# First layer: dense counting up to chunk 1150 instead of 1000, flushed in groups of four tiles instead of twenty

## What is computed

```
head = entity_emb[edge_index[0]]          # source
tail = entity_emb[edge_index[1]]          # destination
att_scores = sigmoid(concat(head, rel[edge_type]) @ att_w + att_b)
aggr_emb = segment_sum(att_scores * tail, edge_index[0], num_segments=N)
out = tanh(aggr_emb @ W_w.T + W_b)
x = layernorm(x + out)
```

## Time and profile before

| | before |
|---|---|
| median of three runs | 11344.98 us (11343.02 to 11346.07) |
| the profiled execution | 11343.15 us |
| its span, first to last instruction | 11341.4 us |
| first layer's indirect DMAs on POOL (L681) | 2125, from 143.6 to 4116.6 us |
| busy share of the span | PE 72%, DVE 68%, ACT 47%, POOL 74% |
| TensorE's granted clock, mean | 0.787 |

### The profile page before, as it was taken

How to read it: one execution, slowest core, us unless ns; L and a number is a source line. 1 busy time by engine, 2 the same in 40 slices (tenths; PEclk the granted TensorE clock), 3 DMA queues, 4 the chain that set the end, 5 groups by cost and what they waited for, 6 DMA issues and landing times. The chain is left out here.

```text
span 11341.4 us, 169992 instructions
## 1 busy us (share of the span) xinstructions
PE 8140.4 (72%) x50598; PEld 5841.4 (52%) x50599; DVE 7676.4 (68%) x18686; ACT 5286.9 (47%) x11630; POOL 8397.3 (74%) x7474
## 2 busy tenths in 40 slices
PE   3777777767777744555656679888888698888887
PEld 2545555555555532444545555555545555555445
DVE  6776666666665538866666559877776598777765
ACT  2644444434333314443333338765544387655442
POOL 4888888888888845777777737777777577777775
PEclk6756666666666656777787869999999799999997
DMA  5343333333333331111111111111111111111111
GB/s 146 37 48 39 38 37 38 38 38 39 38 39 38 39 71 45 29 29 29 29 29 28 27 28 30 30 29 29 29 28 27 35 30 29 30 29 29 28 27 32
DMA packets 690515, 416.79 MB, mean 37 GB/s; under 512 B 488171, under 2 KB 599947, under 8 KB 688344
## 3 DMA queue, kind: packets, MB, share of 16 engines
q0 software_dynamic: 479520, 263.96, 17.9%
q1 hardware_dynamic: 209208, 141.70, 4.7%
q10 hardware_dynamic: 880, 0.23, 0.0%
HBM read 294.68 MB, written 110.67 MB: 36 GB/s over the span
## 5 line engine op out<-in xcount | busy, mean ns | idle before, releaser
L744 POOL DMA_INDIRECT mem<-xt,mem x5325 | 5042.0, 947 | 1680.6 <-issue 1619.7
L681 POOL DMA_INDIRECT table<-mem,idx x2125 | 3305.8, 1556 | 741.9 <-issue 636.6
L1048 PE MATMUL ps<-mem 128*128 128x392 f32 (+5 forms) x6750 | 2707.5, 518 | 224.0 <-DVE mem L1561 106.5
L1561 DVE TENSOR_SCALAR mem<-ps,mem 128x392 f32<-128x392 f32 (+5 forms) x4050 | 2459.2, 627 | 0.0
L1575 DVE TENSOR_TENSOR mem<-mem,ps 128x392 f32 (+2 forms) x3150 | 1805.4, 573 | 851.3 <-PE ps L1048 631.3
L867 ACT ACTIVATE mem<-iota_f,mem 128x128 f32<-128x128 f32 x4050 | 1272.4, 390 | 2242.8 <-PE ps L1048 2231.8
L1081 PE MATMUL ps<-mem 128*64 128x64 f32 (+1 forms) x10650 | 954.8, 243 | 1468.0 <-DMA mem<-xt,mem 1467.3
L1060 PEld LDWEIGHTS ps<-mem,xs 128*64 128x64 f32 (+1 forms) x16464 | 1606.1, 152 | 495.9 <-issue 461.2
L1081 PEld LDWEIGHTS ps<-mem 128*64 128x64 f32 (+1 forms) x10650 | 800.0, 153 | 1958.9 <-DMA mem<-xt,mem 1864.4
L1060 PE MATMUL ps<-mem,xs 128*64 128x94 f32 (+1 forms) x16464 | 1758.6, 265 | 4.5 <-DVE acc L1581 4.5
L1048 PEld LDWEIGHTS ps<-mem 128*128 128x128 f32 (+1 forms) x6750 | 1094.9, 180 | 890.3 <-issue 428.8
(11 more groups left out here) (172 smaller groups left out, 7509.4 us busy)
## 6 DMA issues: line engine op xcount, KB each, us to landing
mem<-xt,mem POOLq DMA_INDIRECT x5325, 2.4
mem<-key_rows SPq DMA_DIRECT2D x425, 160.0 KB, 3.3
table<-mem,idx POOLq DMA_INDIRECT x2125, 3.1
table<-mem POOLq DMA_DIRECT2D x3, 6304.0 KB, 41.0
mem<-table SPq DMA_DIRECT2D x42, 448.0 KB, 5.2
mem<-in_x_dram SPq DMA_DIRECT2D x403, 16.0 KB, 2.0
xt<-xs SPq DMA_DIRECT2D x6, 1024.0 KB
mem<-in_x_dram SPq DMA_DIRECT2D x300, 1.2 KB
```

The costliest lines, as they stand in the source:

```text
L681: pool.indirect_dma_start(out=tables[i % NTAB][:, :], out_offset=bass.IndirectOffsetOnAxis(ap=idx[:, i % (IDXS * GC):i % (IDXS * GC) + 1], ...
L744: pool.indirect_dma_start(out=gbuf[:, o:o + F], out_offset=None, in_=xt[l][:, :], in_offset=bass.IndirectOffsetOnAxis(ap=src_q[q % 2].bitc ...
L1048: last = pe.matmul(ps_d[b % PSD][:, 0:w], lo_l[:, r * P:(r + 1) * P], blk_l[:, r * DT:r * DT + w], start=(k == 0), stop=(k == parts - 1))
L1561: ins = v.tensor_scalar(blk_l[:, r * DT:r * DT + w], iota_p[:, 0:w], kd_q[q % 2][:, at + k:at + k + 1], None, ALU.is_equal)
```

## The change

`C0` rises from 1000 to 1150 and `UZ` falls from 5 to 1; the cost of a zone in the call of `slots` goes from 11.0 to 2.2, so that the cost of a unit stays 2.2. A small row of segment bases moves (32 instead of 64 elements behind its neighbour), with an assertion that all fits.

```
-C0 = 1000
+C0 = 1150
 G00 = C0 // GC
 NT0 = NG - G00
...
-UZ = 5
+UZ = 1
...
 BLOCK0_END, ZONE0_END = slots(SEG_OF0, [0.13 * k * d + 0.24 * d for (_, k), d in zip(BLOCKS[:NB0], ROWS_OF)],
-                              11.0, NU // UZ, NT0, 8)
+                              2.2, NU // UZ, NT0, 8)
...
-        sbase, sbase0 = arena[0:1, rows1:rows1 + NSEG], arena[0:1, rows1 + 64:rows1 + 64 + NS0]
+        sbase, sbase0 = arena[0:1, rows1:rows1 + NSEG], arena[0:1, rows1 + 32:rows1 + 32 + NS0]
...
+        assert NSEG <= 32 and NS0 <= 32 and rows1 + 32 + NS0 <= 8455
```

## The result

The changed kernel takes 12,088 us (median of 4 runs, 12,021 to 12,144) where the kernel before takes 11,346: the ratio is 1.065 (95% interval 1.061 to 1.070). The forecast was 12,790, range 11,600 to 13,000. The direction and the lost overlap hold; the loss is 743 us where 1,446 were forecast, since TensorE's clock was not the forecast one. The time lies near the rival called a mix (12,240), to which the prediction gave 0.14.

A forecast was written before the change was run, and what follows sets the result against it. POOL's indirect DMAs bound the kernel before. Changed, flush phases (PE, 3,263 us), block phases (DVE, 2,097) and 59 make a stage of 5,419 against 3,973: +1,446 on 11,343 gives 12,790 us, range 11,600 to 13,000.

The forecast's parts named there:

- the lost overlap: Flush phases: PE waits for ACT's copy in each unit, 3.43 us instead of 2.56 at half clock, 2.16 instead of 1.33 at full.
- a mix: Rival for the flush phases: half the units at each clock level, about 12,240 us; chance 0.14.
- The bound moves: First layer's stage: POOL no longer sets the pace; the stage is the sum of block and flush phases, 5,419 us.
- Block phases: DVE's one-hots, adds, `keys0`, register loads and handovers, plus iterations without dense work, sum to 2,097 us.
- The clock: Flush phases: the gap in each unit keeps PE's clock at half, making a unit 1.3 us longer.
- half clock throughout: Forecast case: all flush phases at PE's half clock, 3,263 us in sum, kernel 12,790 us; chance 0.60.
- slow starts: Term of the full-clock rival: 4 us at the start of flushing in each of 32 segments, 128 us.
- The prediction's own signs: POOL waits for ACT's copy, last indirect DMA near 5,560 us, PEclk near 0.5 in flush phases, `turn` to `turn` about 3.4 us.
- The full clock throughout: Rival: flush phases at PE's full clock, stage 4,312 us, kernel about 11,680 us; chance 0.14.
- POOL as the bound: Rival: DVE and PE stay under 9.2 us per iteration, kernel 11,063 us, not slower; chance 0.10.

The follow-up runs named there:

- the order alone undone: Changed kernel with PE issuing the next unit's transposes ahead of this unit's multiplications within an iteration: 11,144 us, ratio 0.983 to the kernel before.
- the filled gap: Changed kernel with three extra 128x128 identity multiplications between each unit's transposes and multiplications: 11,610 us, ratio 1.024 to the kernel before.
- a longer gap: Changed kernel with ACT clearing the unit before ahead of copying this one, instead of after: ratio 1.069 to the kernel before.
- a plan for the shorter unit: Kernel with transposes one unit ahead, planner's cost of a unit lowered from 2.2 to 1.4: 11,090 us, ratio 0.977 to the kernel before.

## Why the prediction was right, and where it was off

**The bound moves.** Right. POOL goes from waiting for little but "issue" to 1,156 us of waiting for ACT's copy, and the stage is the sum of its phases: 2,655 and 1,893 us, with 226 us ahead of the first block and 66 behind the last flush, make 4,841. In the prediction's terms, from the first indirect DMA on, the stage is 4,696 us where 5,419 were forecast. Of the 723 us too many 608 are the flush phases' (3,263 forecast, 2,655 measured), 75 the block phases' and 41 the rest.

**Block phases.** Right. Forecast were 2,097 us with 129 for iterations without dense work, 1,968 without them; measured 1,893. A block of 5 rows, for which no row stood, took 1.73 us (the median from one add to the next with a one-hot between) where 1.74 was taken. An add and a one-hot follow each other at the same 1.4 us as in the earlier trace rows:

```profile
2898.05 0.97 DVE L1345 TENSOR_TENSOR mem<-mem,ps 128x784 f32 x1 [1.15 <-PE ps L936]
2898.94 0.62 DVE L1320 TENSOR_SCALAR mem<-ps,mem 128x392 bf16<-128x392 f32 x1
2899.48 1.02 DVE L1345 TENSOR_TENSOR mem<-mem,ps 128x784 f32 x1
```

**The lost overlap.** Right, and shown by the order alone undone: 944 us. The terms are 3.61 us instead of 3.43 at the half clock and 2.27 instead of 2.16 at the full. The difference lies between L959 and the next transposes, 1.87 us (2956.20 to 2958.07) where 1.70 was read in the earlier trace rows. There 1.70 belongs to multiplications that had not waited; those that had waited for ACT stand there too, and take 1.86 us to the next transposes (2120.82 to 2122.68). In the new chain every unit's multiplications wait, so that row was the one to take; in the earlier trace rows it is 1.00 (2131.99 to 2132.99) and not 0.89.

**The clock.** Here the step failed: "So I take the half clock for the flush phases." Each phase begins there, but it rises within the phase. At the half clock throughout, 32 phases were forecast to take 3,263 us, 102 each. That the longest took 101.9 is chance: its last 12 us were at the full clock, and with the measured 3.61 us for a unit the same sum is 3,401, 106 each. At the full clock 2,156 with slow starts were forecast (67 each; the shortest took 67 to 70). Measured were 2,655, with half of the time at each level. The prediction's own signs say the same: the last indirect DMA was to come near 5,560 us and came at 4,841, and PEclk did not stay near 0.5.

The loss that the clock adds to the lost overlap is at least the 479 us that the filled gap gives back, and not the 1,100 forecast. The reading behind it was that a fuller stretch (88% busy) stayed at 0.50 and that the rise in the flush phase followed a run with no gap. Both rows are true, and neither is a rule: a longer gap brings the rise sooner on average, and one multiplication in each gap, which leaves 0.45 us of it, brings it within 7 us of the start. The row at 0.99, from 2125 to 2142 us, also stopped too early. In the same flush phase of the kernel before, the clock fell just behind it:

```profile
2114.70:2195.00 80.30, 59.45 (x415) 55.56 (x414) 34.10 (x130) 33.52 (x48) 66.84 (x43) 0.76 0.37 37
2142.40:2152.60 10.20, 5.95 (x28) 5.55 (x27) 2.85 (x14) 2.56 (x5) 8.37 (x7) 0.50 0.46 54
```

In each of the 23 flush phases measured there the clock rose and fell again, with means of 0.72 to 0.83. So the trace before held a mix already, though PE's idle times in it were others; it spoke against one level throughout as the likeliest case. The rise did not take "some 4 us" each time either: in the kernel before the first rise came 3 to 14 us into a phase. With the gap filled or with the transposes one unit ahead it came after 2 to 6 us, so as a term for the slow start the 4 us hold.

**Luck.** The forecast case, half clock throughout, did not occur. The measured time lies in the range because the range was drawn to take in the mix and the full clock.

**The rule of the Trainium skill.** The Trainium skill, "TensorE: Matmul & The Clock Gate", section "A second HAM failure mode: psum-queue depth-cycling", says that small idle times between groups of matmuls make the clock go back and forth. The trace agrees in the outcome, a mix of both levels with 0.68 us of idle time in each unit: in 14 of the 32 phases the clock fell again for 5 us or more after it had risen. In the other 18 it rose and then held, but for under 5 us.

**The rivals.** The full clock throughout (11,680) is close to what the filled gap gives, 11,610. POOL as the bound (11,063) needs the overlap and a plan for the shorter unit, and is then nearly reached: 11,090.

**Open.** What decides where in a flush phase the clock rises. Idle time of 0.68 us a unit gives 67 to 102 us, 1.19 us gives 80 to 94, and 0.45 or less, with the chain as it is, gives 67 to 71. It is not the idle time alone; what else it is these runs don't show. How much of the 944 us that the overlap brings comes from the clock and how much from the shorter chain is bounded only by the filled gap: 479 by the clock at the old chain, some 466 by the chain at the full clock.

## What to carry to other kernels

When a loop works one step ahead within a unit of scheduling, making that unit smaller can remove the overlap altogether; write the look-ahead over the steps of an iteration, not over those of a zone, and look at the order of instructions, which shows this at once. When a clock level is read for a forecast, read it over whole phases and not over the stretch in which it holds. When work is moved under a bound engine, compare each phase of the others with the bound's pace, since phases that depend on each other don't lend each other time beyond what is buffered. Change a planner's cost together with the time of the step that it stands for.

## What was not expected of the hardware

The granted clock rose in each flush phase of the changed kernel at a place that differed, and in 14 of 32 fell again; equal work took 70 to 102 us, and runs of one kernel spread over 1%. Three multiplications of the identity in each gap of 0.68 us, or a single one, took the phases to 67 to 71 us and the spread to 0.04% or 0.06%, and made the kernel 479 us faster (three; a single one 464, on another chip). A gap made longer by 0.5 us in each of 800 units cost the stage only some 124 us, since the clock rose earlier; why it did stays open.
